# A one-layer transformer tower on one core: where ScalarE switches its function tables around the feed-forward's gelus

## The reference, cut to what matters

```python
h = gelu_tanh(codebook[x] @ W1 + b1) @ W2 + b2          # per token, 256 wide
n = layernorm(h)                                        # first 128 columns: tokens, last 128: positions
att = q @ k.T / 8 + slope * (i - j), causal             # per head, 512 x 512
e = exp(att - max(att)); att = e / (1 + sum(e))
h = h + concat(att @ v) @ Wo
n = layernorm(h)
h = h + gelu_tanh((n @ U1) @ V1 + c1) @ U2 @ V2 + c2    # rank 64, 1024 inner columns
```

## Time and profile before

| | |
|---|---|
| median of 3 runs | 937.65 us (937.57 to 938.27) |
| profiled execution | 937.74 us |
| its span, first to last instruction | 935.9 us |
| mean granted TensorE clock | 0.995 of full |
| busy share of PE, ACT, DVE, POOL | 93%, 78%, 65%, 59% |
| chain that ended last: PE, ACT, DVE, issue | 55%, 13%, 10%, 8% |

### The profile page before, as it was taken

The page is one execution under the profiler, slowest core; times in us unless marked ns, Lnnn a source line. Parts: engine busy times, 40 slices in busy tenths (PEclk is TensorE's granted clock), DMA queues, the critical chain, the costliest instruction groups (busy, mean ns, idle before and its releaser), DMA issues.

```text
span 935.9 us, 16997 instructions
## 1 busy us (share of the span) xinstructions
PE 873.0 (93%) x5660; PEld 680.2 (73%) x5660; DVE 609.7 (65%) x1907; ACT 727.7 (78%) x1622; POOL 555.1 (59%) x471
## 2 busy tenths in 40 slices
PE   7999977999989999999999999999899999999997
PEld 6888856677865786578767876777667866787585
DVE  5565636777685759476848685767757685768434
ACT  6855347998689869897889788877988689869843
POOL 6000067778575867577656767586758575757530
PEclk9999999999999999999999999999999999999999
DMA  9333360001000200020000100010001000000000
GB/s 258 79 113 113 115 197 6 1 1 57 2 1 1 79 1 2 1 59 21 1 1 25 57 1 1 23 58 1 1 23 57 2 1 1 23 2 1 1 23 23
DMA packets 23605, 33.56 MB, mean 36 GB/s; under 512 B 2608, under 2 KB 20176, under 8 KB 23520
## 3 DMA queue, kind: packets, MB, share of 16 engines
q1 hardware_dynamic: 19760, 19.01, 6.3%
q0 software_dynamic: 3760, 13.48, 5.1%
HBM read 17.80 MB, written 14.68 MB: 35 GB/s over the span
## 4 chain that ended last, share of the span: by engine, by line
PE 55%; ACT 13%; DVE 10%; issue 8%; DMA 0%; POOL 0%; DVEq 0%; POOLq 0%; ACTq 0%
PE ps L1202 15%; PE ps L1399 12%; PE ps L1383 9%; PE ps L1370 6%; DVE probs L995 5%; PE ps L1371 5%; ACT turned_sb L830 5%; ACT probs L823 5%; PE ps L1350 4%; ACT k_hi L845 1%; ACT q_both L840 1%; PE ps L1344 1%; DVE q_both L1016 1%; PE ps L1210 1%; DVE stats L960 1%
## 5 line engine op out<-in xcount | busy, mean ns | idle before, releaser
L784 POOL TENSOR_SCALAR probs<-probs,sums 128x512 f32<-128x512 f32 (+2 forms) x384 | 472.6, 1247 | 215.1 <-DVE sums L1002 213.8
L995 DVE CUSTOM_DVE_ANT_0 probs<-ps,causal,slope 128x512 f32<-128x512 f32 (+3 forms) x512 | 268.8, 545 | 143.0 <-PE ps L1371 141.9
L823 ACT ACTIVATE probs<-probs 128x513 f32<-128x513 f32 (+3 forms) x512 | 284.3, 557 | 37.0 <-DVE probs L995 30.4
L1370 PE MATMUL ps<-k_hi,q_both 128*128 128x512 f32 (+3 forms) x512 | 180.9, 353 | 20.7 <-DVE probs L995 18.8
L830 ACT ACTIVATE turned_sb<-ps 128x1280 f32<-128x1280 f32 x128 | 157.1, 1227 | 53.2 <-PE ps L1383 53.2
L1399 PE MATMUL ps<-turned_sb,token_rows 128*64 128x512 f32 (+3 forms) x1024 | 152.0, 438 | 11.8 <-ACT turned_sb L830 11.8
L1383 PE MATMUL ps<-ident,probs 128*128 128x128 f32 x1280 | 161.6, 274 | 0.0
L1371 PE MATMUL ps<-k_lo,q_both 128*128 128x512 f32 (+3 forms) x512 | 152.4, 323 | 0.0
L1399 PEld LDWEIGHTS ps<-turned_sb,token_rows 128*64 128x64 f32 x1024 | 75.2, 136 | 96.7 <-issue 79.3
L1383 PEld LDWEIGHTS ps<-ident,probs 128*128 128x128 f32 x1280 | 143.6, 141 | 0.4 <-issue 0.2
L1370 PEld LDWEIGHTS ps<-k_hi,q_both 128*128 128x128 f32 x512 | 96.3, 188 | 64.2 <-DVE probs L995 37.7
(11 more groups left out here) (226 smaller groups left out, 1463.0 us busy)
## 6 DMA issues: line engine op xcount, KB each, us to landing
out_dram<-token_rows SPq DMA_DIRECT2D x7, 512.0 KB, 2.9
token_table<-made SPq DMA_DIRECT2D x4, 768.0 KB, 4.0
rows<-in_L_tok_codebook_dram SPq DMA_DIRECT2D x4, 512.0 KB, 11.1
w_f<-in_L_tok_W_dram SPq DMA_DIRECT2D x8, 256.0 KB, 5.5
early_rows<-made SPq DMA_DIRECT2D x4, 512.0 KB, 3.0
early_values<-xn SPq DMA_DIRECT2D x4, 512.0 KB, 3.0
token_table<-xn SPq DMA_DIRECT2D x4, 512.0 KB, 4.8
wo_f<-in_L_attn_Wo_dram POOLq DMA_DIRECT2D x1, 1024.0 KB, 11.1
```

The costliest lines, as they stand in the source:

```text
L784: ins = pool.tensor_scalar(at, at, recip[:, s % P_RING, q:q + 1], None, ALU.mult)
L823: act.activation(at, at, ACT.Exp, bias=least, scale=-1.0, accum_out=sums[:, s % P_RING, q:q + 1]).then_inc(exped, 1)
L995: dve.tensor_tensor_reduce(out=probs[:, s % P_RING, start:end], in0=bank(unit % 2)[:, UNIT_AT[q]:UNIT_AT[q] + P * (q + 1)], in1=causal[:, ...
L1370: pe.matmul(dst, w, k_hi[:, slot, 0:P * (q + 1)], start=True, stop=False)
```

## The change

In slot 12 (`burst`), and only there:

- ACT issues a one-column gelu into `spare` behind `exps` 2, ahead of `o_hi`, so that gelu's table is loaded there.
- ACT takes `exps` 3 of this slot's head behind the one-column exponential that follows the eighth gelu, ahead of `z_hi`, instead of ahead of the first gelu.
- In slot 13 DVE does `least_of(s, 0)` ahead of `invert(s - 1)` instead of behind it, because the inverted sums now end later.

```diff
@@ -898,9 +898,12 @@
                 for m in range(1, NT - 1):
                     if s < ALL:
                         exps(s, m)
+                if burst(s):
+
+                    act.activation(spare[:, :], ident[:, 0:1], ACT.Gelu_apprx_tanh)
                 if (s - LAG) % 2 == 0 and 2 + LAG <= s <= ALL + LAG:
                     o_part((s - 2 - LAG) // 2)
-                if s < ALL:
+                if s < ALL and not burst(s):
                     exps(s, NT - 1)
                 for use in second(s):
                     high(*use)
@@ -909,6 +912,7 @@
                     if use[0] == "f" and use[2] == KF - 1 and s < ALL:
 
                         act.activation(spare[:, :], ident[:, 0:1], ACT.Exp)
+                        exps(s, NT - 1)
 
             def y_part(half):
                 act.wait_ge(end_y_full, half + 1)
@@ -1053,9 +1057,11 @@
                 low(*use)
             for s in range(SLOTS):
                 i, j = divmod(s, HEADS)
+                if s < ALL and burst(s - 1):
+                    least_of(s, 0)
                 if 1 <= s <= ALL:
                     invert(s - 1)
-                if s < ALL:
+                if s < ALL and not burst(s - 1):
                     least_of(s, 0)
                 if 1 <= s <= ALL:
                     normalize_first(s - 1)
```

## The result

The changed kernel takes 942.26 us (median of 6 runs, 940.91 to 942.96), the kernel before 937.81 (6 runs, 937.50 to 938.31). The ratio is 1.0045, with a 95% interval of 1.0033 to 1.0057: slower by 0.45%, where 0.3% faster was forecast, and outside the forecast range. The profiled execution took 942.96 us, 5.2 more than the one of before.

What follows compares the result with a forecast made beforehand. PE was busy 93% of the span, but ACT set the burst's start, so the gain was what gelu 4 gains: 7 x 0.39 = 2.7 us off 937.74, giving 935.0 us; 8-in-10 range 933.8 to 936.8.

Steps and rivals of the forecast that it cites:

- step 7: POOL after the burst: late normalising, then c2's addition to 300.6; head ready with 1.4 us to spare, cost nothing.
- the 0.39: Gain per burst in us: f4, and all behind it through slot 13's scores, comes that much earlier.
- rival C: POOL's c2 addition slows beside busy DVE; at twice its time slot 13's head turns 0.95 late, about 941.6; chance 3%.
- rival A: Gain stops at nothing: DVE's scaling pays 0.55 us a burst or f3 waits 0.4 longer; about 937.7; chance 14%.
- Rival B: Slot 13: POOL's widest scaling starts ahead of DVE's and blocks it, 1.41 us a burst, about 945; chance 5%.
- twin row: The last head's scaling on DVE, with no tile between reciprocal and scaling: it took 0.29 us.
- Steps 1 to 3: First burst: gelu 0 0.53 us earlier, o_lo ends at 285.55, f3 newly waits for it, f4 0.39 us earlier.
- Step 5: ACT, burst's end: the fourth exponential, 0.59 us, fits the idle ahead of slot 13's exponential 0, 0.1 to 0.2 spare.
- step 6: DVE in slot 13: reciprocal and hand-over, 0.20 us, are taken in by a 0.36 us idle; cost nothing.

Runs made afterwards that it cites:

- scaling_accum: Changed kernel with only DVE's scaling of slot 13's head written with an added 0 and a row sum put out: 936.55 us, ratio 0.9989.
- c2_first: Changed kernel with POOL's addition of c2 put ahead of the normalising of slot 12's head instead of behind it: 936.22 us, ratio 0.9988.
- early_load_only: Kernel before, with POOL's c2 addition ahead of slot 12's normalising, and exponential 3 then a one-column gelu ahead of o_hi: 945.82 us, ratio 1.0091.

## Why the prediction was wrong

**The step that failed is step 7**, "POOL ... Nothing", and behind it the weighing of the Trainium skill. Step 7 put the addition at 298.3 to 300.6 in slot 14, which is right to about 0.1 us (298.68 to 301.04, less the 0.33 from ahead of the first burst), asked whether anybody waits for POOL, and found 1.4 us to spare, which also held: POOL's normalising holds up no turn. What it didn't ask is what DVE does in those 2.4 us. DVE's scaling of slot 13's head stood in my own rows, at 298.60; less the 0.39 I had given it, 298.2, a tenth of a microsecond ahead of the addition. The rows to look up were on the table.

**The row that I set against the Trainium skill's rule was one of another kind.** I read that a scaling 0.52 us into POOL's scaling took 0.28, and threw out the rule for scalings. I then let the same verdict stand for the addition, which has two operands in SBUF and had never run beside DVE; rival C even says so. The runs show that the kind matters: beside the addition the scaling waits to its end (it took 2.48, or 2.00 from 0.46 us in); beside a one-operand instruction of 1024 columns it took 1.13; 0.5 us into POOL's widest scaling it waits not at all.

The trace of before spoke against my row, too. Of its 128 scalings 47 took over 0.31 us, each with POOL at work beside it. One of them, on DVE and POOL (the second of POOL's two, 1.25 us long, starts at 239.39):

```profile
239.59 0.46 DVE L1008 TENSOR_SCALAR probs<-probs,sums 128x128 f32<-128x128 f32 x1
```
```profile
237.85 2.79 POOL L784 TENSOR_SCALAR probs<-probs,sums 128x512 f32<-128x512 f32 x2 [2.23 <-DVE sums L1002]
```

The 0.837 of the earlier trace rows, from which I took the 0.55 of rival A, starts 0.16 us into a scaling of POOL. So POOL's one-operand instructions hold DVE's scaling up too, but only in their first part, and the row at 298.60 stands 0.52 us in, behind that part.

The Trainium skill, "SBUF — State Buffer", Who interferes with whom, says that GpSimd and a two-port VectorE instruction exclude each other for the whole instruction, without a difference by the kind of GpSimd instruction, and that the scaling form that puts out its accumulator has no two-port mode. For the addition the first half agrees with the changed kernel (2.48); for POOL's one-operand instructions it doesn't, by the 1.13 beside 2.76 us, and there the measurement decides. The second half agrees with scaling_accum (0.34).

**Rival C named the right pair and priced the wrong side.** It asked how much longer c2 would take beside a busy DVE. c2 took 2.36, against 2.37 before; it was DVE that paid. That C's 941.6 lies near the 942.26 measured is luck. Rival B had the right mechanism at the wrong meeting: line 1012 in slot 13 took 0.29, as its twin row said.

**Steps 1 to 3 were right in kind, and one term was mis-sized.** Gelu 0 gained 0.50 for 0.53, PE got a new wait for `o_lo` (0.51), g0 and g1 run as a pair, f4 stands 1.01 behind them. But `o_hi` follows the one-column gelu by 0.21 us where I took 0.11 from `z_hi` behind its twin. That is 0.10 on `o_lo` and f3, and the gain was 0.27 in place of 0.39. The same 0.21 stands in the trace of before, from the sum's reading at 282.63 to the 282.84 I had worked out for `o_hi`: the term was to be had. ACT's idle ahead of gelu 4 grew to 0.91 rather than 0.8 for that reason.

**Step 5 and step 6 held.** The late exponential fits into ACT's idle, which shrank from 0.73 to 0.23. DVE in slot 13 was in time. By c2_first the forecast without its blind spot would have been 1.1 to 1.9 us of gain instead of 2.7, and about at the limit of what can be told.

**The sum that was to be made:** 7 x 0.27 = 1.9 us of gain, against 2.2 of blocking less 1.1 of slack in each of the six bursts where the two meet, 6.6 in all. That is 4.7 slower, 942.5; measured were 942.26.

## What to carry to other kernels

When a change makes an engine's work later, ask not only who waits for it but also what will run beside it then: on VectorE and GpSimd, line up both timelines for the stretch it moves to and look at every pair of SBUF instructions. A rule about pairs is only refuted by a row of the same pair, in operands and in order. And when a table load or any filler is put ahead of a copy, follow the copy to its last reader: here the copy's bank was what TensorE wrote next. The load and its small gelu put `o_hi` 1.5 us later, and only 0.9 us of that were covered (in the trace of before, `o_lo` ended at 284.16 and f3 started at 285.06).

## What the runs showed of the hardware that I had not expected

- A DVE scaling whose record starts 0.02 us *ahead* of POOL's two-operand addition still waits for its end (298.66 against 298.68). The wait shows as a longer instruction, not as idle time, and starts so close together don't tell which of the two gets through; POOL's spans are rough in these profiles.
- A DVE scaling that starts up to 0.43 us into POOL's 512 wide one-operand scaling ends some 0.77 us behind POOL's start, so it takes 0.46 us at 0.31 in and 0.36 at 0.41. From 0.46 us in it takes 0.28 to 0.31, if no other POOL instruction starts beside it. The traces of all the kernels here show this, in over a hundred scalings of the first kind and several hundred of the second, but for one that started 0.04 us in and took 1.65 (scaling_accum). What ends the wait was not settled.
- One row sum put out by the scaling, never used, costs 0.06 us and lets it run beside the addition (0.34 in place of 2.48).
- In the profiled execution of early_load_only, PE's granted clock fell for some microseconds behind the 1.68 us wait of the last burst, and in no other of its bursts though they have the same wait. This kernel's engines in three stretches (busy us and instructions of each, then the granted clock):

```profile
870.00:879.00 9.00, 7.15 (x43) 4.66 (x41) 5.28 (x15) 8.31 (x18) 6.53 (x5) 1.00 0.00 0
879.00:883.00 4.00, 4.00 (x11) 1.64 (x12) 0.00 (x0) 1.72 (x4) 3.17 (x3) 0.57 0.00 0
883.00:890.00 7.00, 6.56 (x35) 3.73 (x31) 2.23 (x10) 6.24 (x12) 0.00 (x0) 1.00 0.00 0
```

  A mean of 0.57 is the lower level of 1.2 GHz for most of the 4 us. That burst's f4 came 0.9 us later than in the others. Whether this is all that lies between the 945.8 measured and the 944 worked out was not settled.
